# Graph attention over 4096 nodes on one core: second PSUM homes for the projections, four output banks, a new order of the setup, and weighing with 512 moving columns

## The reference

```python
h = jnp.maximum(_layernorm(x, axis=-1), 0.0)          # x: 4096 x 256
q = h @ Wq.T + bq;  k = h @ Wk.T + bk;  v = h @ Wv.T + bv
a = q @ k.T / sqrt(256) + adj + adj                   # 4096 x 4096, adj is read: 64 MB
out = x + softmax(a, axis=-1) @ v
```

## Time and profile before

| | |
|---|---|
| three runs | 718.05, 717.42, 718.0 us; median 718.0 |
| profiled execution | 719.87 us, its span 718.1 us |
| PE busy, matmuls | 692.2 us (96%), 4799 |
| PE weight loads | 475.0 us, 4799, beside the matmuls |
| DVE, ACT, POOL busy | 597.3, 436.7, 431.5 us (83%, 61%, 60%) |
| DMA | 161.06 MB, mean 224 GB/s |

### The profile page before, as it was taken

One profiled execution on the slowest core, in us unless ns is written; L12 is line 12 of the kernel. 1 busy time (PEld: TensorE's weight loads), 2 busy tenths in 40 slices (PEclk: granted clock), 3 DMA queues, 4 the chain that ended last, 5 costly groups with the idle time before them and its releaser, 6 DMA issues.

```text
span 718.1 us, 14692 instructions
## 1 busy us (share of the span) xinstructions
PE 692.2 (96%) x4799; PEld 475.0 (66%) x4799; DVE 597.3 (83%) x1282; ACT 436.7 (61%) x732; POOL 431.5 (60%) x436
## 2 busy tenths in 40 slices
PE   5788999999999999999999999999999999999998
PEld 3555555566766666666676666676676676666776
DVE  4889777988888888888788988887887878887895
ACT  4799564565756555656656565656566565656530
POOL 1879603575655667564756565675647475655676
PEclk9999999999999999999999999999999999999999
DMA  8398588998878888887888888888889788888563
GB/s 272 126 284 225 142 225 224 257 252 228 249 211 247 238 237 228 254 222 208 259 228 246 236 250 221 227 224 265 223 221 269 212 238 246 241 220 227 127 167 98
DMA packets 93244, 161.06 MB, mean 224 GB/s; under 512 B 20976, under 2 KB 41840, under 8 KB 93168
## 3 DMA queue, kind: packets, MB, share of 16 engines
q1 hardware_dynamic: 68432, 126.41, 63.1%
q10 hardware_dynamic: 24736, 33.72, 17.6%
HBM read 80.35 MB, written 8.39 MB: 124 GB/s over the span
## 4 chain that ended last, share of the span: by engine, by line
PE 73%; DVE 7%; DMA 6%; SPq 4%; issue 3%; ACTq 3%; ACT 2%; POOL 1%; DVEq 0%; POOLq 0%
PE bank L1448 40%; PE bank L1509 33%; SPq L420 3%; ACTq L789 3%; DMA out_y<-xy 2%; DMA rows<-in_adj 2%; DVE rows L1128 2%; DMA xT<-rows 1%; DVE rows L1101 1%; DVE top L1137 1%; DMA rows<-in_x 1%; DVE stats L1046 1%; ACT rows L709 1%; DVE rows L1079 0%; SPq L372 0%
## 5 line engine op out<-in xcount | busy, mean ns | idle before, releaser
L625 POOL TENSOR_TENSOR wT<-xT,wT 128x512 f16<-128x512 f32 x233 | 268.7, 1162 | 234.4 <-ACT wT L807 230.2
L1448 PE MATMUL bank<-v_sb,wT 128*128 128x256 f16 x2796 | 342.8, 273 | 0.2 <-POOL wT L625 0.2
L1509 PE MATMUL bank<-top,a_op 128*128 128x512 f16 x1344 | 330.8, 379 | 5.3 <-DVE chunk_max L1101 2.3
L1448 PEld LDWEIGHTS bank<-v_sb,wT 128*128 128x128 f16 x2796 | 273.1, 98 | 81.8 <-DVE xy L1191 2.3
L807 ACT CAST wT<-xT 128x512 f16<-128x512 f32 x233 | 139.6, 611 | 126.3 <-PE bank L1448 75.1
L1509 PEld LDWEIGHTS bank<-top,a_op 128*128 128x128 f16 x1344 | 130.7, 98 | 115.7 <-DVE chunk_max L1101 3.6
L778 ACT ACTIVATE rows<-rows,exp_bias,exp_scale 128x1024 f32<-128x1024 f32 x128 | 158.7, 1240 | 66.3 <-issue 37.4
L1101 DVE CUSTOM_DVE_ANT_0 rows<-bank,rows 128x512 f32<-128x512 f32 x256 | 173.4, 679 | 10.7 <-PE bank L1509 2.3
L1128 DVE STREAM_TRANSPOSE rows<-rows 128x1024 f32<-128x1024 f32 x128 | 158.5, 1239 | 6.0 <-ACT rows L778 6.0
L1086 DVE SCALAR_TENSOR_TENSOR rows<-rows,adj_scale,bank 128x512 f32<-128x512 f32 x64 | 47.6, 744 | 48.3 <-PE bank L1509 48.3
L769 ACT ACTIVATE rows<-rows,adj_scale 128x512 f32<-128x512 f32 x64 | 46.2, 722 | 32.9 <-POOL wT L625 21.0
(11 more groups left out here) (115 smaller groups left out, 457.6 us busy)
## 6 DMA issues: line engine op xcount, KB each, us to landing
rows<-in_adj SPq DMA_DIRECT2D x128, 512.0 KB, 5.4
xT<-rows SPq DMA_DIRECT2D x488, 64.0 KB, 2.9
xT<-rows ACTq DMA_DIRECT2D x488, 64.0 KB, 3.3
rows<-in_x SPq DMA_DIRECT2D x8, 512.0 KB, 6.0
xy<-in_x SPq DMA_DIRECT2D x32, 128.0 KB, 5.2
g_scratch<-xT SPq DMA_DIRECT2D x16, 256.0 KB, 3.6
g_pair<-g_scratch SPq DMA_DIRECT2D x15, 256.0 KB, 3.9
out_y<-xy SPq DMA_DIRECT2D x30, 128.0 KB, 5.7
```

The costliest lines, as they stand in the source:

```text
L625: nc.gpsimd.tensor_tensor(split_piece(m, 1), exchanged(m), split_piece(m, 0), ALU.subtract).then_inc(split_lo, 1)
L1448: return nc.tensor.matmul(out_ap, stationary, moving, start=first, stop=last)
L1509: last = nc.tensor.matmul(ps[:], s, mv, start=first and k == 0, stop=k == 2, skip_group_check=True)
```

## The change

Four things are done.

1. Weighing: for all tiles but the last (`WIDE_TILES` = 31) the two matmuls of the high weights become one, with 512 moving columns: the high and the low half of V lie side by side in `v_sb`, and the result takes the whole bank, low part on the right. Low weights x high V still adds to the left half. Before `finish`, a new `add_low` on VectorE adds the scaled right half to the output row.
2. The output has four banks (4 to 7, by tile % 4), and the first weighing of a tile waits for `finish` of the tile four before it. `finish` moves from the end of a period to behind `turn(u, 0)`, with `add_low` ahead of that turn.
3. Projections have second homes: `project_g` in bank 6 and, for one step, bank 2, later banks 6 and 5 in turn; `project_v` in banks 7 and 1, later 4 and 7 in turn. Each waits only for the reads of the last one in its own bank.
4. The setup of all five engines is written in another order; two low keys, (0, T2) and (2, T4), go from GpSimd to VectorE.

```diff
+WIDE_TILES = TILES - 1
 HIGH_ORDER = (
-    (0, B11), (0, B21), (0, T1), (0, B22), (0, T3), (0, T2), (0, T4),
+    (0, B11), (0, B21), (0, T1), (0, B22), (0, T2), (0, T3), (0, T4),
...
-        o_ps = bank[4:6]
+        o_banks = bank[4:8]
-        g_ps = bank[6]
-        v_ps = bank[7]
+        g_homes = (6, 2, 6, 6) + (6, 5) * 6
+        v_homes = (7, 1, 7, 1, 7, 7, 7, 7, 7) + (4, 7) * 3 + (7,)
...
+        def used_before(homes, k):
+            return max((j + 1 for j in range(k) if homes[j] == homes[k]), default=0)
+        def out_bank(tile):
+            return o_banks[tile % 4]
...
# SP: the first loads
             load_x(1)
             load_x(2)
+            load_xy(0)
+            load_rows(0)
+            load_rows(1)
+            load_rows(2)
             load_x(3)
...
# GpSimd
             key_sum_t2(0)
+            layernorm_factors(2)
             key_sum_t4(0)
             pool_low_key(0, T1)
-            layernorm_factors(2)
+            layernorm_factors(3)
             pool_low_key(0, T3)
-            layernorm_factors(3)
+            query_sums(0)
             layernorm_factors(4)
-            pool_low_key(0, T2)
-            query_sums(0)
             layernorm_factors(5)
...
# VectorE
-            def finish(tile):
+            def add_low(tile):
+                if tile >= WIDE_TILES:
+                    return
...
+                nc.vector.scalar_tensor_tensor(y, out_bank(tile)[:, D:2 * D], out_scale[:, t:t + 1], y,
+                                               ALU.mult, ALU.add).then_inc(low_added, 1)
+
+            def finish(tile):
+                t = tile % 2
+                if tile < WIDE_TILES:
+                    dve.wait_ge(low_added, tile + 1)
...
+            statistics(2)
             nc.vector.scalar_tensor_tensor(fold[:, 3], wvT_ps[:, 0, :], wv_scale[:], fold[:, 1],
                                            ALU.mult, ALU.add).then_inc(folded, 1)
-            statistics(2)
...
             low_key(0, B22)
-            low_v(0)
             statistics(5)
             low_key(0, T4)
+            low_v(0)
+            low_v(1)
...
# VectorE, in a period
+                done = 2 * p - 6 + n % QUADS
+                if n % QUADS >= 2 and p >= 2:
+                    add_low(done)
                 turn(u, 0)
+                if n % QUADS >= 2 and p >= 2:
+                    finish(done)
...
-                if n % QUADS == 2 and p >= 2:
-                    finish(2 * p - 4)
-                if n % QUADS == 3 and p >= 2:
-                    finish(2 * p - 3)
...
# VectorE, the tail: sums and finish of tiles 28 and 29 go behind the last turns
             turn(u + 1, 1)
-            sums(TILES - 4)
             late_high(LATE + 4)
             late_high(LATE + 5)
-            finish(TILES - 4)
+            sums(TILES - 4)
             late_high(LATE + 6)
-            sums(TILES - 3)
...
# TensorE
             def project_g(g, c):
-                wait(pe, g_evicted, DC * g + c)
+                wait(pe, g_evicted, used_before(g_homes, DC * g + c))
...
             def project_v(unit):
-                wait(pe, v_lo_done, unit)
+                wait(pe, v_lo_done, used_before(v_homes, unit))
...
-                        wait(pe, y_done, 2 * p + t - 1)
+                        wait(pe, y_done, 2 * p + t - 3)
...
-                    matmul(o_ps[t][:, 0:D], w_hi, v_sb[:, kt, 0], half == 0 and block == 0, False)
-                    matmul(o_ps[t][:, 0:D], w_hi, v_sb[:, kt, 1], False, False)
+                    if 2 * p + t < WIDE_TILES:
+                        matmul(out_bank(2 * p + t)[:], w_hi, v_sb[:, kt].rearrange("p s d -> p (s d)"), first, False)
+                    else:
+                        matmul(out_bank(2 * p + t)[:, 0:D], w_hi, v_sb[:, kt, 0], first, False)
+                        matmul(out_bank(2 * p + t)[:, 0:D], w_hi, v_sb[:, kt, 1], False, False)
...
# TensorE, the order from quarter 2 on
-            product_5(2)
             project_v(8)
             product_7(2)
             product_2(2)
             project_g(2, 0)
+            product_5(2)
+            project_v(9)
+            product_3(2)
             product_2(3)
-            product_3(2)
-            project_v(9)
+            project_v(10)
             product_6(3)
```

More of the change, by code:

```diff
@@ L1215, in _ @@
             last.then_inc(bk_widened, 1)
+            statistics(1)
             dve.wait_ge(m_done, 1)
@@ L1308, in _ @@
             low_v(6)
+            finish_22(1)
             low_key(2, B22)
-            finish_22(1)
+            low_v(7)
             finish_21(1)
             finish_11(1)
-            low_v(7)
             low_key(3, B21)
             finish_12(1)
+            scores_12(2)
             row_bias(0)
-            scores_12(2)
             scores_11(3)
-            low_key(3, B22)
             row_bias(1)
@@ L1323, in _ @@
             finish_22(2)
+            low_key(3, B22)
             low_v(8)
+            finish_12(2)
             finish_11(3)
-            finish_12(2)
+            low_v(9)
+            scores_12(3)
             row_bias(2)
-            scores_12(3)
-            low_v(9)
+            low_key(2, T4)
             scores_22(3)
@@ L1335, in _ @@
             low_v(11)
+            finish_21(2)
             turn(0, 0)
-            finish_21(2)
             turn(0, 1)
-            low_v(12)
             finish_21(3)
@@ L1342, in _ @@
             scores_11(4)
-            turn(1, 0)
+            low_v(12)
             low_v(13)
             scores_12(4)
+            turn(1, 0)
+            low_v(14)
             scores_11(5)
             turn(1, 1)
-            low_v(14)
             scores_22(4)
+            finish_22(4)
             low_v(15)
-            finish_22(4)
+            scores_12(5)
             turn(2, 0)
-            scores_12(5)
             finish_21(4)
@@ L1621, in _ @@
             transpose_h(3, 0)
+            project_v(3)
             transpose_h(3, 1)
-            project_v(3)
+            transpose_h(4, 0)
             product_1(0)
-            transpose_h(4, 0)
             transpose_h(4, 1)
+            product_5(0)
             project_v(4)
@@ L1629, in _ @@
             product_1(1)
-            product_5(0)
             product_7(0)
```

276 lines of the change are left out of this document (150 added, 126 removed).

## The result

| | before | after |
|---|---|---|
| median of 20 runs each | 718.63 us (717.42 to 719.93) | 716.74 us (712.58 to 719.62) |
| ratio | | 0.9966, 95% interval 0.9954 to 0.9977 |
| profiled execution, its span | 719.87, 718.1 us | 717.0, 715.3 us |
| PE busy, matmuls | 692.2 us, 4799 | 688.9 us, 3807 |
| DVE, ACT, POOL busy | 597.3, 436.7, 431.5 us | 595.4, 436.0, 428.9 us |

The account below looks back on a forecast made before the run. TensorE was taken to bound the kernel from the first weighing on, with 10.1 us of idleness in the setup. Setup 5.0 + wide weighing 2.5 + tail 0.7 - slips 0.5 = 7.7 us, so 718.0 becomes 710.3 us, range 705.5 to 714.8.

Parts of the forecast that it names:

- The setup: Setup before the first weighing: new banks and order bring PE there 5.0 us earlier; bounds 2 and 11.3 us.
- (a): Setup, project_g(0, 1): writes bank 2, so it follows project_g(0, 0) at 25.4 us and not at 30.13.
- (b): Setup, transpose_h(2): factors at 24.3, transposes at 29.5; PE idles 2 us where it idled 4.55.
- the walk: Setup chain from trace durations, (a) to (e): PE 5.0 us ahead at product_6(3), carried over to the weighing.
- (c): Setup, project_v(2): waits for low_v(0) alone, starts near 34.1 us, 3.2 us ahead of 37.27.
- (d): Setup, project_v(5): by the same walk comes at 45.9 us against 49.59, 3.7 us ahead.
- (e): Setup, product_6(3): with two low keys fewer on POOL, at 71.3 us against 75.01, project_v(10) done, 5.0 us ahead.
- the lead given back at the change to the steady state: Rival, chance 0.17: only 2 of the setup's 5 us remain, 713.3 us; ScalarE's first cast waits for a DMA.
- The wide weighing: Weighing of 31 tiles: 992 pairs become single 512-column matmuls, 2.5 ns each, 2.5 us; bounds 0 and 2.5.
- 0.28 us of cover: Steady state: scores_22 slips 0.66 us, still ends 0.28 us before product_4; 0.5 us booked for slips, bounds 0 and 5.6.
- the slower rival: Steady state, chance 0.04: VectorE's inserted operations make scores_22 late and product_4 waits; 14 us lost, 723.8 us.
- The tail: Kernel's end: waits of 0.40 us for finish and 0.30 for the last low halves go, 0.7 us; bounds 0 and 0.7.

Follow-up runs that it names:

- e4: The changed kernel with x's group 3 loaded ahead of the first adjacency loads, as before the change; 716.41 us, ratio 0.9959 to the kernel before.
- e5: e3 with, in periods n % 4 = 0, loads of x's tile and g behind the exchange and adjacency loads; 720.17 us, ratio 1.0023.
- e6: e3 with add_low moved behind turn(u, 0); 714.05 us, ratio 0.9925 to the kernel before.
- e11: e10 with narrow weighing, every tile by 256-column pairs (WIDE_TILES = 0); 713.34 us, ratio 0.9925 to the kernel before.
- e12: e10 with low_v(0) two steps earlier in VectorE's setup, ahead of statistics(5) and low_key(0, T4); 713.12 us, ratio 0.991.
- e2: The changed kernel with narrow weighing (WIDE_TILES = 0), so without add_low; 716.02 us, ratio 0.9954 to the kernel before.
- e3: The changed kernel with the first adjacency load, refill(1, 0), put between exchange_a(1) and exchange_a(2); 715.9 us, ratio 0.9951.
- e10: e6 with the output stores one period earlier, as in e9; 712.66 us, ratio 0.9913 to the kernel before.
- e9: The changed kernel with output stores one period earlier, behind the finish that makes the row; 714.57 us, ratio 0.9929.

## Why the prediction was wrong

**The setup (5.0 booked, 3.2 measured at the first weighing, 1.7 left at C, four periods on).** Steps (a) and (b) held: `project_g(0, 1)` follows at once, the transposes wait 1.65 us (2 in the walk), with full clock behind them in this trace (in those of e4, e5 and e6 it fell there, and A to B was not longer for it). Step (c) did not: `project_v(2)` starts 35.70 - 13.90 = 21.8 us behind the first transposes, 24.1 before, a lead of 2.3 where 3.2 stood; at `project_v(5)` (d) it is 2.9 for 3.7, at `product_6(3)` (e) 4.3 for 5.0, with `project_v(10)` counted in. Over the eleven traces of the new setup up to e11, A to B lies between 98.31 and 99.14 us, and 102.12 and 102.77 in the two of the old: 3.7 us between the middles. e12 shows, up to the half clock in its trace, what was wrong with the walk. It moved one TensorE step at a time to where its own producer let it go and carried the lead on; but ScalarE and VectorE fill this stretch, and a wait taken away from one product stands before the next. And the first transposes start 12.44 to 13.90 us into the twelve traces of the changed setup, by when x and the biases land: 1.5 us of chance, under which the walk's last digits drown.

**"From there to the weighing PE was busy throughout ... so I carry the 5.0 us over" is the step that failed.** It was busy there only in the trace of before. With the lead PE caught up with VectorE: 1.1 us went at three waits before the first weighing ("PE idle before the first weighing" was one of the prediction's own signs of being wrong), and 1.5 us more between B and C. I saw the rival that fits (the lead given back at the change to the steady state, 713.3 us) and gave it 0.17, with the wrong place: not ScalarE's first cast but the adjacency of period 8. The diff showed SyncE issuing `exchange_a(2)` ahead of `refill(1, 0)`, and I had weighed SyncE's order for x alone. The late load cost 2.54 us of idleness (1.02 before) and 1.7 us of half clock, of which the clock is in part luck: e2 idled 2.56 us in the same place without it. With the load put first the idleness is 1.75 us or less in eight traces, and no row there is slow. B to C is 1.6 to 2.7 us shorter in e3, e6 and e10, but only 0.4 in e12, where the next load, that of period 10, is late in its turn (PE idles 1.34 us at 147.09).

**The wide weighing (2.5 booked).** The price per pair was right: 2.5 ns worked out, 2.3 measured in e11 against e10, in traces where PE waits for nothing from C to D. Of the 1.9 us that the pairs are worth from C to D, 1.5 came. The changed kernel lost 2.2 us there against e9, but the kernel before was already losing: it took 509.87 us, and e11, with the same narrow weighing and no load late from C to D, 508.16. "PE busy 100 of 100 us" hid this. And I read the 1.9 us for L1079 in the earlier trace rows as "spread over the steady state", which is wrong: 1.02 of it is the wait at 128.13, in period 8, at the very place where I then let the lead pass for nothing. Only 0.63 and 0.21 us are in the steady state, in periods 26 and 42. The loads stood in VectorE's list, late in three periods, and there the faster TensorE made them eight.

**`add_low` (0.28 us of cover, 0.5 booked).** `product_4` never waited for `scores_22`, and the slower rival with its 14 us didn't come. VectorE's timeline of a period with an `add_low` (L1209), and PE's `product_4` behind it, against the earlier trace rows:

```profile
393.37 0.75 DVE L1102 SCALAR_TENSOR_TENSOR rows<-rows,adj_scale,bank 128x512 f32<-128x512 f32 x1 [1.17 <-PE bank L1547]
...
394.64 0.48 DVE L1209 SCALAR_TENSOR_TENSOR xy<-bank,out_scale,xy 128x256 f32<-128x256 f32 x1
395.04 1.23 DVE L1144 STREAM_TRANSPOSE rows<-rows 128x1024 f32<-128x1024 f32 x1
...
396.56 0.73 DVE L1110 SCALAR_TENSOR_TENSOR rows<-rows,adj_scale,bank 128x512 f32<-128x512 f32 x1
```
```profile
397.71 0.81 PE L1547 MATMUL bank<-top,a_op 128*128 128x512 f16 x3
```

`scores_22` starts 3.19 us behind `scores_12` (2.67 before; 3.33 worked out) and ends at 397.29, 0.42 us ahead of `product_4`, without a gap on PE. The cover held. What I didn't follow is the turn. The turn releases the exchange, the exchange stands ahead of the adjacency loads on SyncE, and so 0.4 us on VectorE (the first turn 1.67 us behind `scores_12` where it was 1.27) made the loads of two periods in four 0.4 us later. e6 took that back. Its ratio is 0.0026 below e3's, 1.9 us, but with intervals that overlap and only 0.2 us between their traces from C to D, so what those 0.4 us cost is not shown.

**The tail (0.7 booked)** gave 0.45. The wait of 0.40 us in the earlier trace rows is gone and one of 0.31 stands, in PE's timeline:

```profile
686.85 25.11 PE L1480 MATMUL bank<-v_sb,top 128*128 128x256 f16 x180 [0.31 <-POOL top L643]
```

**The account.** Booked: 5.0 + 2.5 + 0.7 - 0.5 = 7.7. Found: 3.2 - 1.5 + 1.5 + 0.45 - 0.8 = 2.9 in the traces, 1.9 between the medians. Of the 4.8 us that are missing, 0.7 are the setup's walk, 1.1 the lead lost between it and the first weighing, 1.5 the lead given back behind the weighing, and 0.8 the late start, which is chance. 1.0 and 0.25 are missing from the wide weighing and the tail, against 0.5 booked for slips that did not come. With the load order mended (e10) the kernel is 6.0 us faster than before (718.68 - 712.66). That is not the proof that all the gains priced here were there, since e10 also wins what the kernel before was losing from C to D, 1.7 us by the comparison with e11.

## What to carry to other kernels

Where the bounding engine is at 100%, look up each of its small recurring waits by its place in time, and read the list of waits of the engine that it waits for, down to the queue that issues the transfer: here loads that were late in three periods of the steady state were late in eight after the change. A load that waits for a store's landing holds up everything behind it in its queue; issue the store earlier, before moving the load later, since a load moved back only finds another engine waiting. And when a step is moved or inserted on one engine, follow what it releases down to the last DMA queued behind that.

## What the runs showed of the hardware

Behind idleness of 2.54 us in the middle of a busy stretch TensorE's clock stood at 0.50 (after, until 130), and so it did behind 3.27 us (e4, 126.07) and 3.69 us (e9, 126.23). Behind 1.70 us (e3), 2.15 us (e5, at 148.44) and 2.56 us (e2, at 125.37) no row was slow. Yet in e12 the clock fell behind 2.45 us (36.82), and in e4 and e5 behind 2.1 and 1.4 us in close succession (28.7 and 31.1). So the length of one stretch of idleness doesn't decide it in these traces, and the 1.7 us that half clock cost in period 8 can come or not with the same wait. In the changed kernel the clock was also at 0.50 from 12 to 24 us:

```profile
16.00:20.00 4.00, 1.77 (x9) 0.50 0.67 200
```

and yet A to B took 98.94 us, within the 98.31 to 99.14 of the other traces, e3 and e10 with the clock at 1.00 there among them: in that stretch TensorE isn't the bound. The changed kernel's runs scattered by 7 us (712.58 to 719.62), those before by 2.5 beside them, but by 7.1 in the rounds of e9 to e11 (716.65 to 723.7), where e9 to e11 themselves scattered by 3.9, 3.8 and 3.4.
